# Adding the two expert rows on GpSimd, and storing the last tile in two parts

## The chip, the core and the metric

The kernel runs on one core of a Trainium2 chip. The metric is the device time of one execution, in microseconds; smaller is better. Engines go by their names in the profile: PE is TensorE (PEld its weight loads), DVE is VectorE, ACT is ScalarE, POOL is GpSimd, SP is SyncE, which here only issues DMAs.

## What is computed

One transformer block with adaptive layer norm: attention over 8 sequences of 1024 tokens with 128 features, then a mixture of 8 experts of which each token uses two, and one shared expert that every token uses. The part that matters here is the end:

```
h = relu(einsum('td,edf->tef', xf, W1) + b1)
sparse = einsum('te,tef,efd->td', combine, h, W2) + combine @ b2
shared = relu(xf @ Ws1 + bs1) @ Ws2 + bs2
x = x + gb * (sparse + shared)          # gb: one gate row for each of the 8 sequences
```

Everything is float32. `combine` has two values that are not zero in each row, so `sparse` is a sum of two expert rows per token.

## The kernel before

Tokens are laid out as 8 batches (`B`) of 1024 tokens (`S`); a batch is 8 groups (`G`) of 128 rows. In SBUF a batch of results, `res`, is 128 partitions x 1024 numbers. A tile is 512 tokens, half a batch; `K` = 4 groups.

After attention, token rows are scattered by expert to DRAM, run through the experts tile by tile, weighted, and scattered back to `rows_z` in DRAM by GpSimd's indirect DMAs (line 780, the last four on line 794). `rows_z` holds two rows for each token: the first expert's and the second's. The shared expert runs in tiles of its own, eight of them before the expert tiles and eight (batches 4 to 7, `i` = 0 to 7) after them. Those last eight tiles and the gathering of `rows_z` are the **last stage**, from about 599 us to the end.

In the last stage SP loads `rows_z` batch by batch into SBUF slots (`load_results`, line 464). A slot holds `z0`, the first experts' rows, and `z1`, the second experts' rows. The order of batches is 4, 0, 5, 1, 6, 2, 7, 3; the first half of batch 4 has a load of its own. There are six slots, and the loads of batches 7 and 3 are issued only after the third store (line 471), since they reuse the slots of batches 4 and 0.

TensorE makes a shared tile in two steps: `last_up(i)` (lines 1731 to 1733, into `score`) and `last_down(i)` (line 1940, into one of three PSUM banks `yacc`, called value or misc in the profile). ScalarE applies relu (line 967) and copies the next input (line 957, `h_hi`), VectorE makes the low part of the next input (line 1271, `last_x`), and then TensorE can start the next `last_up`.

VectorE does all the finishing, in an order written out by hand: `rows_into_result(0)`, `add_front(0)`, `last_x(5)`, `add_shared(1)`, `add_shared(2)`, `last_x(6)`, `add_front(1)`, `last_x(7)`, `add_shared(3)`, `add_shared(4)`, `add_front(2)`, `add_shared(5)`, `add_front(3)`, `add_shared(6)`, `add_last_shared(7)`. For a half batch with a shared tile (`add_shared`) these are four instructions of 128x512: PSUM + z0 (line 1640), + z1 (line 1642), times the gate `mod` (line 1643), into `res` (line 1644). For a batch without one (`add_front`, the shared part was added earlier) three of 128x1024: z0 + z1 (line 1652), gate (line 1653), into `res` (line 1654). Each waits for the one in front of it by a semaphore (`fin`). SP stores each piece when it is ready. No GpSimd instruction stands in the last stage: its last is an indirect DMA on line 794.

Of the kernel before, what the change touches and what calls it, by code (L numbers as in the profile page):

```python
# [34 lines left out]
P = 128  # L35
B, S, D = 8, 1024, 128
G = S // P
# [73 lines left out]
def adaln_moe(nc, x, c_t, wmod, w_att, b_att, wg, packs, out):  # L111
    with ExitStack() as ctx:
# [6 lines left out]
        def sem(name):  # L119
            return ctx.enter_context(nc.semaphore(name))  # L120
# [226 lines left out]
        y_sent = [sem(f"y_sent{i}") for i in range(RING)]  # L347
        z_loaded = [sem(f"z_loaded{i}") for i in range(B)]
        fin_step = sem("fin_step")
        bias_step = sem("bias_step")  # L350
# [12 lines left out]
        z_slot = {b: z_at[i % len(z_at)] for i, b in enumerate(z_order)}  # L363
        fin_parts = [p for i in range(B // 2 - 1) for p in ((B // 2 + i, 0), (i, None), (B // 2 + i, 1))]
        fin_parts += [(B // 2 - 1, None), (B - 1, 0), (B - 1, 1)]

# [24 lines left out]
        def _(sp):  # L391
# [74 lines left out]
            def store(i):  # L466

                b, half = fin_parts[i]
                sp.wait_ge(fin_ready, i + 1)
                at = slice(0, G) if half is None else slice(half * K, half * K + K)  # L470
                sp.dma_start(out_v[b, :, at.start * D:at.stop * D],
                             res[:, b * G + at.start:b * G + at.stop, :].rearrange("p g d -> p (g d)")).then_inc(stored, 16)

# [14 lines left out]
        def _(pool):  # L488
# [567 lines left out]
        def _(dve):  # L1056
# [565 lines left out]
            def rows_into_result(i):  # L1622
# [7 lines left out]
                nc.vector.tensor_tensor(r, r, z0, ALU.add).then_inc(fin_ready, 1)  # L1630

            def add_shared(i):

                b, half = divmod(FRONT + i, 2)
                dve.wait_ge(z_loaded[b], 16)
                dve.wait_ge(down_ready, FRONT + ROW_TILES + i + 1)
                z0, z1 = (z_slot[b][:, k * S + half * TILE:k * S + half * TILE + TILE].rearrange("p (g d) -> p g d", d=D) for k in range(2))
                gate = mod[:, b:b + 1, 4, :].to_broadcast([P, K, D])
                r = res[:, b * G + K * half:b * G + K * half + K, :]
                nc.vector.tensor_tensor(z0, yacc[(i + 2) % RING].rearrange("p (k d) -> p k d", k=K), z0, ALU.add).then_inc(y_evac, 1)  # L1640
                dve.wait_ge(y_evac, FRONT + ROW_TILES + i + 1)
                fin(nc.vector.tensor_tensor(z0, z0, z1, ALU.add))  # L1642
                fin(nc.vector.tensor_tensor(z0, z0, gate, ALU.mult))  # L1643
                nc.vector.tensor_tensor(r, r, z0, ALU.add).then_inc(fin_ready, 1)  # L1644

            def add_front(b):

                dve.wait_ge(z_loaded[b], 16)
                z0, z1 = (z_slot[b][:, k * S:(k + 1) * S].rearrange("p (g d) -> p g d", d=D) for k in range(2))
# [15 lines left out]

            def add_last_shared(i):

                b, half = divmod(FRONT + i, 2)
                z0, z1 = (z_slot[b][:, k * S + half * TILE:k * S + half * TILE + TILE].rearrange("p (g d) -> p g d", d=D) for k in range(2))
                gate = mod[:, b:b + 1, 4, :].to_broadcast([P, K, D])  # L1670
                r = res[:, b * G + K * half:b * G + K * half + K, :]
                fin(nc.vector.tensor_tensor(z0, z0, z1, ALU.add))
                fin(nc.vector.tensor_tensor(z0, z0, gate, ALU.mult))
                fin(nc.vector.tensor_tensor(r, r, z0, ALU.add), wait=False)
                dve.wait_ge(down_ready, FRONT + ROW_TILES + i + 1)
                nc.vector.tensor_tensor(z1, yacc[(i + 2) % RING].rearrange("p (k d) -> p k d", k=K), gate, ALU.mult).then_inc(y_evac, 1)
                dve.wait_ge(y_evac, FRONT + ROW_TILES + i + 1)
                dve.wait_ge(fin_step, fin.now())
                nc.vector.tensor_tensor(r, r, z1, ALU.add).then_inc(fin_ready, 1)
# [18 lines left out]
            add_shared(6)  # L1698
            add_last_shared(7)


        @block.tensor
        def _(pe):
# [335 lines left out]
            def last_down(i):  # L2039
                down(FRONT + ROW_TILES + i, w_shared, (i + 2) % RING, part=i % 2, banks=3)  # L2040

            pe.wait_ge(h2t_staged, 2 * B)
            last_up(0)
            last_expert_down()
            for i in range(SHARED_TILES - FRONT):
                if i + 1 < SHARED_TILES - FRONT:
                    last_up(i + 1)
                last_down(i)


# [26 lines left out]
```

## Time and profile before

| | us |
|---|---|
| median of 3 runs | 649.85 (649.65 to 651.14) |
| the profiled execution, its own time | 649.9 |
| its span (first to last instruction) | 648.2 |
| PE busy over the span | 610.2 (94%) |
| DVE busy | 460.7 (71%) |
| POOL busy | 340.9 (53%) |

The profiled execution is one run; its time outside the span is 1.7 us. Busy shares are averages over stages that have different limits, so the last stage has to be read by itself.

### The profile page before, as it was taken

How to read it: one execution, taken by the hardware profiler on the slowest of the kernel's cores; microseconds unless marked ns; L12 is line 12 of the kernel's file. 1: busy time of each engine (PE TensorE's matmuls, PEld its weight loads, DVE VectorE, ACT ScalarE, POOL GpSimd, SP SyncE). 2: the span in 40 equal slices, each digit the busy share in tenths (PEclk: the TensorE clock that was granted, in tenths of full speed). 3: DMA queues.
4: the chain of work that ended last, by engine and by line, in shares of the span. 5: the costliest groups of instructions: out<-in, count | busy, mean ns of one | idle time of the engine just before them, and what ended most of it. 6: DMA issues, size and time to landing. Idle time of an engine off the chain costs nothing.

```text
span 648.2 us, 12495 instructions
## 1 busy us (share of the span) xinstructions
PE 610.2 (94%) x4311; PEld 557.4 (86%) x4311; DVE 460.7 (71%) x1415; ACT 397.6 (61%) x635; POOL 340.9 (53%) x341
## 2 busy tenths in 40 slices
PE   3898999999999998986999999999999999999995
PEld 2587988898889897875998999999999999999995
DVE  7889878798989898996775564544545445453788
ACT  3588787878787876554345555565655656555441
POOL 4531614766666666777560575555655556656000
PEclk9899999999999999997999999999999999999998
DMA  7140000111111111111166456656666566601972
GB/s 296 38 163 2 1 1 10 38 33 34 35 34 34 34 39 35 40 47 45 64 197 201 149 175 207 187 178 199 196 204 198 180 196 194 204 31 34 360 305 113
DMA packets 29902, 76.67 MB, mean 118 GB/s; under 512 B 7126, under 2 KB 11374, under 8 KB 29712
## 3 DMA queue, kind: packets, MB, share of 16 engines
q1 hardware_dynamic: 20480, 58.49, 27.2%
q0 software_dynamic: 8640, 16.93, 7.7%
q8 instruction: 34, 0.56, 0.4%
q10 hardware_dynamic: 720, 0.47, 0.2%
q14 instruction: 28, 0.23, 0.1%
HBM read 53.53 MB, written 23.24 MB: 118 GB/s over the span
## 4 chain that ended last, share of the span: by engine, by line
PE 49%; DVE 3%; issue 1%; ACT 1%; ACTq 0%
PE value L1940 18%; PE misc L1940 7%; PE score L1731 7%; PE score L1733 7%; PE score L1732 7%; PE value L1991 2%; PE misc L1772 1%; PE value L2030 1%; DVE res L1644 0%; DVE rows_all L1155 0%; ACT work L967 0%; DVE rows_all L1642 0%; DVE rows_all L1643 0%; DVE rows_all L1640 0%; DVE w_ring L1653 0%
## 5 line engine op out<-in xcount | busy, mean ns | idle before, releaser
L780 POOL DMA_INDIRECT rows_z<-tile_y,tags x138 | 139.2, 1009 | 115.1 <-DVE tile_y L1560 49.5
L1731 PE MATMUL score<-h_hi,h_lo 128*128 128x512 f32 (+1 forms) x252 | 93.8, 372 | 2.2 <-DVE h_hi L1271 1.9
L1759 PE MATMUL value<-w_ring,work 128*128 128x129 f32 x768 | 92.1, 276 | 1.1 <-ACT work L840 1.0
L1759 PEld LDWEIGHTS value<-w_ring,work 128*128 128x128 f32 x768 | 89.6, 192 | 3.2 <-ACT work L840 1.4
L967 ACT ACTIVATE work<-score,w_ring 128x512 f32<-128x512 f32 (+1 forms) x96 | 53.0, 614 | 60.8 <-PE score L1733 59.2
L1733 PE MATMUL score<-h_hi,h_lo 128*128 128x512 f32 (+1 forms) x252 | 88.7, 352 | 0.0
L1732 PE MATMUL score<-h_hi,h_lo 128*128 128x512 f32 (+1 forms) x252 | 88.4, 351 | 0.0
L576 POOL DMA_INDIRECT rows_x<-work,slot x64 | 65.1, 1017 | 39.7 <-issue 15.5
L838 ACT ACTIVATE work<-work 128x1024 f32<-128x1024 f32 x64 | 67.2, 1050 | 26.4 <-DVE work L1168 26.2
L1168 DVE TENSOR_TENSOR work<-score,lw 128x1024 f32<-128x1024 f32 x64 | 76.6, 1214 | 1.9 <-PE score L1733 1.2
L967 ACT ACTIVATE work<-score,w_shared 128x512 f32<-128x512 f32 x64 | 40.3, 684 | 49.9 <-PE score L1733 48.5
L840 ACT ACTIVATE work<-work 128x1024 f32<-128x1024 f32 x64 | 67.8, 1060 | 2.0
L967 ACT ACTIVATE work<-score,rows_all 128x256 f32<-128x256 f32 (+1 forms) x92 | 43.8, 547 | 38.6 <-PE score L1733 37.8
L1731 PE MATMUL score<-q_hi,h_lo 128*128 128x512 f32 x128 | 54.6, 426 | 5.5 <-DVE work L1168 4.9
L1731 PEld LDWEIGHTS score<-h_hi,h_lo 128*128 128x128 f32 x252 | 47.7, 189 | 7.8 <-DVE rows_all L1177 2.0
L1733 PEld LDWEIGHTS score<-h_hi,h_lo 128*128 128x128 f32 x252 | 47.4, 188 | 6.6
L1732 PEld LDWEIGHTS score<-h_hi,h_lo 128*128 128x128 f32 x252 | 47.7, 189 | 4.9
L1733 PE MATMUL score<-q_hi,h_hi 128*128 128x512 f32 x128 | 50.8, 397 | 0.0
L1732 PE MATMUL score<-q_lo,h_hi 128*128 128x512 f32 x128 | 50.6, 396 | 0.0
L1940 PEld LDWEIGHTS value<-w_shared,work 128*128 128x128 f32 x416 | 49.5, 197 | 1.1 <-ACT work L967 0.5
L1940 PE MATMUL value<-w_shared,work 128*128 128x128 f32 x416 | 50.2, 281 | 0.0
L1275 DVE TENSOR_TENSOR h_lo<-w_ring,h_lo 128x512 fp32r<-128x512 f32 x24 | 16.6, 692 | 43.5 <-ACT h_lo L960 43.5
(254 smaller groups left out, 1270.7 us busy)
## 6 DMA issues: line engine op xcount, KB each, us to landing
w_ring<-packs SPq DMA_DIRECT2D x24, 578.0 KB, 3.9
rows_all<-packs SPq DMA_DIRECT2D x23, 578.0 KB, 3.9
lw<-rows_x SPq DMA_DIRECT2D x24, 260.0 KB, 3.8
res<-x SPq DMA_DIRECT2D x8, 512.0 KB, 6.2
h_t<-rows_z SPq DMA_DIRECT2D x3, 1024.0 KB, 10.4
mod<-mod_rows SPq DMA_DIRECT2D x1, 2560.0 KB, 10.0
rows_z<-tile_y,tags POOLq DMA_INDIRECT x142
rows_all<-rows_z SPq DMA_DIRECT2D x2, 1024.0 KB, 12.9
```

The lines of the kernel that those rows point to most:

```text
L576: nc.gpsimd.indirect_dma_start(rows_x[:, :], bass.IndirectOffsetOnAxis(ap=slot[b % 2][:, k, g:g + 1], axis=0), (rows_1, rows_2)[k][b % 2][ ...
L780: nc.gpsimd.indirect_dma_start(rows_z[:, :], bass.IndirectOffsetOnAxis(ap=tags[pos][:, k, 0:1].bitcast(I32), axis=0), tile_y[par][:, k, :] ...
L838: nc.scalar.activation(prob[:, t % 4, :], prob[:, t % 4, :], ACT.Tanh).then_inc(tanh_done, 1)
L840: nc.scalar.activation(prob[:, t % 4, :], prob[:, t % 4, :], ACT.Exp).then_inc(exp_done, 1)
L967: ins = nc.scalar.activation(hidden[par][:, c, 0:rows], score[:, c, 0:rows], ACT.Relu, bias=w[:, B1_AT + c:B1_AT + c + 1])
L1168: nc.vector.tensor_tensor(prob[:, t % 4, :].rearrange("p (h n) -> p h n", h=2), score[:, 2 * (t % 2):2 * (t % 2) + 2, :], lw[:, at:at + S] ...
L1275: nc.vector.tensor_tensor(w1_lo[par], w[:, 0:F], w1_hi[par].bitcast(F32), ALU.subtract).then_inc(w_split, 1)
L1731: nc.tensor.matmul(out, a_lo, b_hi, start=True, stop=False)
L1732: nc.tensor.matmul(out, a_hi, b_lo, start=False, stop=False)
L1733: return nc.tensor.matmul(out, a_hi, b_hi, start=False, stop=True)
L1759: ins = nc.tensor.matmul(value[:, s // 3, c0:c0 + D + 1], prob[:, t % 4, s * P:(s + 1) * P], normal[b % 3][:, t, :], start=(t == 0 and s % ...
L1940: ins = nc.tensor.matmul(yacc[par][:, k * D:(k + 1) * D], hidden[part][:, c, k * P:(k + 1) * P], w[:, W2_AT + c * D:W2_AT + (c + 1) * D], ...
```

## The change

GpSimd gets eight instructions at the end of its program, `sum_rows`: z0 = z0 + z1 for batch 0, the second half of batch 4, and batches 5, 1, 6, 2, 7, 3, each as soon as its load has landed. VectorE no longer adds z1; it waits for the sum (`z_summed`) instead. (The first half of batch 4, `rows_into_result`, keeps its addition on VectorE.) The last shared tile is made by TensorE in two parts of two groups each, the second into the bank `xt_ps`, which is free by then; VectorE gates, adds and SP stores each part by itself.

```diff
-        fin_parts += [(B // 2 - 1, None), (B - 1, 0), (B - 1, 1)]
+        fin_parts += [(B // 2 - 1, 0, G), (B - 1, 0, K), (B - 1, K, K + 2), (B - 1, K + 2, G)]
...
+            def sum_rows(b, n0=0):
+                pool.wait_ge(z_loaded[b], 16)
+                z0, z1 = (z_slot[b][:, k * S + n0:(k + 1) * S] for k in range(2))
+                nc.gpsimd.tensor_tensor(z0, z0, z1, ALU.add).then_inc(z_summed, 1)
+            sum_rows(z_order[1])
+            sum_rows(z_order[0], TILE)
+            for b in z_order[2:]:
+                sum_rows(b)
...
+            def summed(b):
+                dve.wait_ge(z_summed, 1 + (z_order[1:2] + z_order[0:1] + z_order[2:]).index(b))
...
             def add_shared(i):
-                dve.wait_ge(z_loaded[b], 16)
+                summed(b)
...
                 nc.vector.tensor_tensor(z0, yacc[(i + 2) % RING].rearrange("p (k d) -> p k d", k=K), z0, ALU.add).then_inc(y_evac, 1)
                 dve.wait_ge(y_evac, FRONT + ROW_TILES + i + 1)
-                fin(nc.vector.tensor_tensor(z0, z0, z1, ALU.add))
                 fin(nc.vector.tensor_tensor(z0, z0, gate, ALU.mult))
                 nc.vector.tensor_tensor(r, r, z0, ALU.add).then_inc(fin_ready, 1)
...
             def add_front(b):
-                dve.wait_ge(z_loaded[b], 16)
+                summed(b)
...
-                fin(nc.vector.tensor_tensor(z0, z0, z1, ALU.add))
                 fin(nc.vector.tensor_tensor(z0, z0, gate, ALU.mult))
                 nc.vector.tensor_tensor(r, r, z0, ALU.add).then_inc(fin_ready, 1)
...
+            def last_shared_part(i, part, bank):
+                dve.wait_ge(*((down_ready, FRONT + ROW_TILES + i + 1) if part else (part_ready, 1)))
+                n = K // 2
+                gated = nc.vector.tensor_tensor(z1, bank[:, 0:n * D].rearrange("p (k d) -> p k d", k=n), mod[:, b:b + 1, 4, :].to_broadcast([P, n, D]), ALU.mult)
+                gated.then_inc(part_evac, 1)
+                dve.wait_ge(part_evac, part + 1)
+                nc.vector.tensor_tensor(r, r, z1, ALU.add).then_inc(fin_ready, 1)
...
-            add_last_shared(7)
+            last_rows_into_result(7)
+            last_shared_part(7, 0, yacc[(7 + 2) % RING])
+            last_shared_part(7, 1, xt_ps)
```

On VectorE, from the finishing of batch 0 (`add_front(0)`) to that of the second half of batch 4 (`add_shared(1)`), before (h2_t, which the profile calls h_t, is where the slots of batches 4 and 0 lie):

```order
L1652 TENSOR_TENSOR h2_t<-h2_t 128x1024 [waits z_loaded0]
L1653 TENSOR_TENSOR h2_t<-h2_t,mod 128x1024 [waits fin_step]
L1654 TENSOR_TENSOR res<-res,h2_t 128x1024 [waits fin_step]
L1271 TENSOR_TENSOR h_hi0<-h2_t,h_hi0 128x512 [waits x_hi_ready]
L1640 TENSOR_TENSOR h2_t<-value,h2_t 128x512 [waits down_ready,z_loaded4]
L1642 TENSOR_TENSOR h2_t<-h2_t 128x512 [waits y_evac]
L1643 TENSOR_TENSOR h2_t<-h2_t,mod 128x512 [waits fin_step]
L1644 TENSOR_TENSOR res<-res,h2_t 128x512 [waits fin_step]
```

The same place after the change:

```order
L1669 TENSOR_TENSOR h2_t<-h2_t,mod 128x1024 [waits z_summed]
L1670 TENSOR_TENSOR res<-res,h2_t 128x1024 [waits fin_step]
L1285 TENSOR_TENSOR h_hi0<-h2_t,h_hi0 128x512 [waits x_hi_ready]
L1658 TENSOR_TENSOR h2_t<-value,h2_t 128x512 [waits down_ready,z_summed]
L1660 TENSOR_TENSOR h2_t<-h2_t,mod 128x512 [waits y_evac]
L1661 TENSOR_TENSOR res<-res,h2_t 128x512 [waits fin_step]
```

One instruction of each group is gone, and the first of each group waits for GpSimd's sum and no longer for the load. On GpSimd, what stands at the end of the program after the change, behind the last indirect DMAs:

```order
L796 DMA rows_z<-tile_y1,tags4 16384x128 [waits y_ready]
L804 TENSOR_TENSOR h2_t<-h2_t 128x1024 [waits z_loaded0]
L804 TENSOR_TENSOR h2_t<-h2_t 128x512 [waits z_loaded4]
L804 TENSOR_TENSOR work<-work 128x1024 [waits z_loaded5]
L804 TENSOR_TENSOR rows_all<-rows_all 128x1024 [waits z_loaded1]
L804 TENSOR_TENSOR rows_all<-rows_all 128x1024 [waits z_loaded6]
L804 TENSOR_TENSOR w_ring<-w_ring 128x1024 [waits z_loaded2]
L804 TENSOR_TENSOR h2_t<-h2_t 128x1024 [waits z_loaded7]
L804 TENSOR_TENSOR h2_t<-h2_t 128x1024 [waits z_loaded3]
```

Before, the program ended with the DMA. On VectorE, the end of the program, before:

```order
L1672 TENSOR_TENSOR h2_t<-h2_t 128x512
L1673 TENSOR_TENSOR h2_t<-h2_t,mod 128x512 [waits fin_step]
L1674 TENSOR_TENSOR res<-res,h2_t 128x512 [waits fin_step]
L1676 TENSOR_TENSOR h2_t<-value,mod 128x512 [waits down_ready]
L1679 TENSOR_TENSOR res<-res,h2_t 128x512 [waits fin_step,y_evac]
```

and after:

```order
L1688 TENSOR_TENSOR h2_t<-h2_t,mod 128x512 [waits z_summed]
L1689 TENSOR_TENSOR res<-res,h2_t 128x512 [waits fin_step]
L1699 TENSOR_TENSOR h2_t<-value,mod 128x256 [waits part_ready,fin_step]
L1702 TENSOR_TENSOR res<-res,h2_t 128x256 [waits part_evac]
L1699 TENSOR_TENSOR h2_t<-value,mod 128x256 [waits down_ready]
L1702 TENSOR_TENSOR res<-res,h2_t 128x256 [waits part_evac]
```

The addition is gone, and the two last instructions of 128x512 are four of 128x256.

## Rows read from the trace of the kernel before

**Rows 1.** Stretches: length, busy of PE, PEld, DVE, ACT, POOL; clock, DMA, GB/s
```profile
606.20:621.20 15.00, 15.00 (x100) 13.60 (x100) 14.56 (x18) 7.30 (x12) 0.00 (x0) 1.00 1.02 406
621.20:623.20 2.00, 2.00 (x20) 2.00 (x19) 0.04 (x2) 1.85 (x4) 0.00 (x0) 1.00 1.02 416
623.20:645.70 22.50, 17.90 (x136) 16.75 (x134) 21.83 (x28) 5.07 (x8) 0.00 (x0) 0.96 0.39 156
```

**Rows 2.** Timeline of DVE in the last stage: start, length, engine, line
```profile
617.48 1.22 DVE L1652 TENSOR_TENSOR rows_all<-rows_all 128x1024 f32<-128x1024 f32 x1
618.73 1.23 DVE L1653 TENSOR_TENSOR rows_all<-rows_all,mod 128x1024 f32<-128x1024 f32 x1
...
623.18 0.69 DVE L1271 TENSOR_TENSOR h_hi<-h_t,h_hi 128x512 fp32r<-128x512 f32 x1 [1.96 <-ACT h_hi L957]
623.79 0.68 DVE L1640 TENSOR_TENSOR work<-misc,work 128x512 f32<-128x512 f32 x1
624.51 0.69 DVE L1642 TENSOR_TENSOR work<-work 128x512 f32<-128x512 f32 x1
625.23 0.69 DVE L1643 TENSOR_TENSOR work<-work,mod 128x512 f32<-128x512 f32 x1
...
644.27 0.68 DVE L1676 TENSOR_TENSOR h_t<-value,mod 128x512 f32<-128x512 f32 x1
644.99 0.69 DVE L1679 TENSOR_TENSOR res<-res,h_t 128x512 f32<-128x512 f32 x1
```

**Rows 3.** Timeline of PE: the last shared tile's down projection
```profile
637.37 3.74 PE L1940 MATMUL value<-w_shared,work 128*128 128x128 f32 x32
```

**Rows 4.** Timelines of POOL and DVE, 46 to 52 us
```profile
46.99 4.70 POOL L550 TENSOR_TENSOR res<-res,mod 128x1024 f32<-128x1024 f32 x2
...
48.15 1.24 DVE L1075 SCALAR_TENSOR_TENSOR shift<-moments,rstd 128x8 f32<-128x8 f32 x1
49.32 1.21 DVE L1168 TENSOR_TENSOR work<-score,lw 128x1024 f32<-128x1024 f32 x1
50.45 1.28 DVE L1075 SCALAR_TENSOR_TENSOR shift<-moments,rstd 128x24 f32<-128x24 f32 x1
```

**Rows 5.** Lengths of single lines over the whole span, min/median/max ns
```profile
L1075 DVE SCALAR_TENSOR_TENSOR shift<-moments,rstd x5: 167/383/1281, 10.1 to 85.3; 128x8 f32<-128x8 f32 x3, 128x24 f32<-128x24 f32 x1, 128x16 f32<-128x16 f32 x1
...
L554 POOL TENSOR_SCALAR rstd<-moments x8: 238/534/583, 67.8 to 295.9; 128x8 f32<-128x8 f32 x8
```

**Rows 6.** Timeline of DVE and POOL around 99 us
```profile
99.34 0.66 DVE L1116 TENSOR_TENSOR h_lo<-tile_y,h_hi 128x512 fp32r<-128x512 f32 x1
...
99.61 0.49 POOL L554 TENSOR_SCALAR rstd<-moments 128x8 f32<-128x8 f32 x1 [16.55 <-DVE moments L1065]
```

**Rows 7.** Lengths of POOL's 128x1024 additions, min/median/max ns
```profile
L550 POOL TENSOR_TENSOR res<-res,mod x8: 2367/2381/2399, 47.0 to 247.3; 128x1024 f32<-128x1024 f32 x8
...
L571 POOL TENSOR_TENSOR row<-row,mod x1: 2192/2192/2192, 75.2 to 75.2; 128x1024 f32<-128x1024 f32 x1
```

**Rows 8.** Timeline of DVE: a 128x256 read of PSUM in the expert stage
```profile
591.65 0.42 DVE L1603 TENSOR_TENSOR tile_y<-value,rows_all 128x256 f32<-128x256 f32 x1 [2.92 <-PE value L2030]
592.11 0.48 DVE L1608 TENSOR_SCALAR tile_y<-tile_y,tags 128x128 f32<-128x128 f32 x2
```

**Rows 9.** DMA issues in the last stage: count, KB, us to landing
```profile
h_t<-rows_z SPq DMA_DIRECT2D x1, 1024.0 KB, 6.0
...
w_ring<-rows_z SPq DMA_DIRECT2D x1, 1024.0 KB, 17.1
...
h_t<-rows_z SPq DMA_DIRECT2D x1, 1024.0 KB, 10.4
...
out<-res SPq DMA_DIRECT2D x1, 256.0 KB, 2.0
```

**Rows 10.** Timeline of SP: issues of the loads in the last stage
```profile
599.75 1.43 SPq L464 DMA_DIRECT2D h_t<-rows_z  x3
...
602.82 0.52 SPq L464 DMA_DIRECT2D w_ring<-rows_z  x1
```

More of the change, by code:

```diff
@@ L466, in store @@
             def store(i):
-                b, half = fin_parts[i]
+                b, g0, g1 = fin_parts[i]
                 sp.wait_ge(fin_ready, i + 1)
-                at = slice(0, G) if half is None else slice(half * K, half * K + K)
-                sp.dma_start(out_v[b, :, at.start * D:at.stop * D],
-                             res[:, b * G + at.start:b * G + at.stop, :].rearrange("p g d -> p (g d)")).then_inc(stored, 16)
+                sp.dma_start(out_v[b, :, g0 * D:g1 * D],
+                             res[:, b * G + g0:b * G + g1, :].rearrange("p g d -> p (g d)")).then_inc(stored, 16)
             load_results(z_order[0], z_half_loaded, 0, TILE)
@@ L1664, in _, with last_rows_into_result @@
             last_expert()
-            def add_last_shared(i):
+            def last_rows_into_result(i):
                 b, half = divmod(FRONT + i, 2)
-                z0, z1 = (z_slot[b][:, k * S + half * TILE:k * S + half * TILE + TILE].rearrange("p (g d) -> p g d", d=D) for k in range(2))
-                gate = mod[:, b:b + 1, 4, :].to_broadcast([P, K, D])
+                summed(b)
+                z0 = z_slot[b][:, half * TILE:half * TILE + TILE].rearrange("p (g d) -> p g d", d=D)
                 r = res[:, b * G + K * half:b * G + K * half + K, :]
[L1672 to L1678, printed above, removed]
+                fin(nc.vector.tensor_tensor(z0, z0, mod[:, b:b + 1, 4, :].to_broadcast([P, K, D]), ALU.mult))
+                fin(nc.vector.tensor_tensor(r, r, z0, ALU.add))
+            def last_shared_part(i, part, bank):
+                b, half = divmod(FRONT + i, 2)
+                dve.wait_ge(*((down_ready, FRONT + ROW_TILES + i + 1) if part else (part_ready, 1)))
+                n = K // 2
+                z1 = z_slot[b][:, S + part * n * D:S + (part + 1) * n * D].rearrange("p (g d) -> p g d", d=D)
+                g0 = b * G + K * half + n * part
+                r = res[:, g0:g0 + n, :]
+                gated = nc.vector.tensor_tensor(z1, bank[:, 0:n * D].rearrange("p (k d) -> p k d", k=n), mod[:, b:b + 1, 4, :].to_broadcast([P, n, D]), ALU.mult)
+                gated.then_inc(part_evac, 1)
+                dve.wait_ge(part_evac, part + 1)
                 nc.vector.tensor_tensor(r, r, z1, ALU.add).then_inc(fin_ready, 1)
@@ L2040, in last_down, with last_down_in_parts @@
                 down(FRONT + ROW_TILES + i, w_shared, (i + 2) % RING, part=i % 2, banks=3)
+            def last_down_in_parts(i):
+                n = FRONT + ROW_TILES + i
+                pe.wait_ge(y_evac, n - 2)
+                pe.wait_ge(hidden_ready, HALVES * (n + 1))
+                for part, bank in enumerate((yacc[(i + 2) % RING], xt_ps)):
+                    for c in range(C):
+                        for k in range(K // 2):
+                            at = (K // 2 * part + k) * P
+                            ins = nc.tensor.matmul(bank[:, k * D:(k + 1) * D], hidden[i % 2][:, c, at:at + P],
+                                                   w_shared[:, W2_AT + c * D:W2_AT + (c + 1) * D],
+                                                   start=(c == 0 and k == 0), stop=(c == C - 1), skip_group_check=True)
+                    ins.then_inc(down_ready if part else part_ready, 1)
             pe.wait_ge(h2t_staged, 2 * B)
@@ L2044, in _ @@
             last_expert_down()
-            for i in range(SHARED_TILES - FRONT):
-                if i + 1 < SHARED_TILES - FRONT:
-                    last_up(i + 1)
+            for i in range(SHARED_TILES - FRONT - 1):
+                last_up(i + 1)
                 last_down(i)
+            last_down_in_parts(SHARED_TILES - FRONT - 1)
 def kernel(**inputs):
```

9 lines of the change are left out of this document (6 added, 3 removed).

## The prediction

> **What bounds the kernel now.** I first cut the last stage into stretches [rows 1]. TensorE is busy throughout until about 641 us; VectorE is busy for 14.56 of 15 us, then idle for 2 us (it waits for ScalarE, which follows TensorE's pace), then busy for 21.83 of the last 22.5 us. GpSimd does nothing. So from 623.2 us on VectorE sets the end, and before that it is just in time. Its timeline says the same [rows 2]: the 1.96 us wait in front of line 1271 is the last idle time, and from there to 645.68 (644.99 + 0.69) each instruction starts as soon as the one before it lets it. The last matmul group ends at 637.37 + 3.74 = 641.1 us [rows 3], 4.6 us before VectorE is done. After VectorE comes only the last store, 2.0 us [rows 9], and 0.5 us to the end of the span at 648.2.
>
> VectorE work removed after 623.2 us is therefore worth its full time until TensorE's end is reached; work removed before it only widens the idle time, unless something has filled that up.
>
> **What the change removes.** Steps are counted from start to start [rows 2]. A 128x512 addition on line 1642 takes 625.23 - 624.51 = 0.72 us; there are six of them and one like them on line 1672. A 128x1024 addition on line 1652 takes 618.73 - 617.48 = 1.25 us; there are four. Together 7 x 0.72 + 4 x 1.25 = 10.0 us. Of this 4 x 0.72 + 2 x 1.25 + 0.72 = 6.1 us stand behind 623.2.
>
> **What it adds on VectorE.** Now two last instructions take 0.72 + 0.69 = 1.41 us. Two parts take, with 0.42 us for a 128x256 instruction and 0.46 from its start to a next one that waits for it [rows 8], and 0.08 us less than its length where the next one does not wait (623.18 to 623.79 is 0.61 against 0.69 [rows 2]): 0.46 + 0.34 + 0.46 + 0.42 = 1.68, so +0.27. In front of them one `res` addition is now waited for, 0.72 in place of 0.61: +0.11. Sum +0.4 us. It buys something only if VectorE reaches the last tile before TensorE does.
>
> **What it adds on GpSimd, and the main term.** Seven sums of 128x1024 and one of 128x512. The nearest rows are GpSimd's own 128x1024 float32 additions: 2.38 us in one form, 2.19 in another [rows 7]. Neither has two plain operands; I take 2.3 and keep both ends. The half sum is not in the trace; it lies between half of 2.3 and all of it, and I take 1.25, near the half, since most of such a length should go with the elements.
>
> On the face of it these 17.4 us run beside VectorE. The trace says they do not. At 48.15 us VectorE starts a tiny instruction, 128x8 from two SBUF tensors, while GpSimd's addition runs. It takes 1.24 us [rows 4]; the shortest on that line takes 0.167 [rows 5]. It ends at 49.39, and GpSimd's first addition ends at 46.99 + 2.35 = 49.34. The next one at 50.45 takes 1.28 us and ends at 51.73; GpSimd's second addition ends at 51.69. Between them, under the second of these GpSimd additions, VectorE multiplies 128x1024 numbers from PSUM with others from SBUF in 1.21 us (line 1168) and is not held up [rows 4]. So an instruction of VectorE with two SBUF inputs waits until GpSimd's is over, and one with an input in PSUM does not. The reverse is there as well: GpSimd's line 554 takes 0.49 us when it starts under a 128x512 VectorE subtraction from SBUF that ends at 100.00 [rows 6], and 0.238 alone [rows 5]; it ends 0.10 us after VectorE's.
>
> The Trainium skill has this as a rule ("SBUF — State Buffer", section "SBUF: two separate sides"): VectorE and GpSimd share a pair of SBUF ports that is locked for a whole instruction, against VectorE instructions with two SBUF inputs too. By that rule the trace agrees, in both directions. Its "GPSIMD Engine Reference", section 3.1, gives 4497 ns for an addition of 2048 float32; half of that, an estimate of 2.25 us, would make the sum 0.35 us smaller.
>
> In the last stage only lines 1640 and 1676 read PSUM. Everything else on VectorE (lines 1271, 1643, 1644, 1653, 1654, and what is left of the rest) has two SBUF inputs.
>
> Price of one sum in a dense stretch: it gets in at the gap between two VectorE instructions. GpSimd's record then ends 0.10 + 2.3 - 0.24 = 2.16 us after the VectorE record in front of it; the next VectorE instruction begins its work 0.13 us before that (51.69 against 51.73 - 0.167 = 51.56 [rows 4, 5]), in place of 0.03 us after its predecessor. Loss 2.16 - 0.13 - 0.03 = 2.0 us. Half sum 0.95. Three of the eight meet a VectorE instruction that would have overlapped its predecessor by 0.08, +0.3 in all. Eight sums: 7 x 2.0 + 0.95 + 0.3 = 15.25 us.
>
> What covers them: each time a line-1640 instruction (0.72 us a step) falls under a sum, that much is not lost. I laid the two programs side by side, each taking turns, with the loads landing as now: batch 0 is there at 606.2 (the second of three issues from 599.75 on, at about 600.2, and 6.0 us), batch 2 at 602.8 + 17.1 = 619.9 [rows 9, 10], the other three between. Two of the sums, those of batches 6 and 7, fall on a line-1640 instruction: -1.4 us. The idle 1.96 us at 621.2 is eaten: -1.96.
>
> **Sum.** -10.0 + 0.4 + 15.25 - 1.4 - 1.96 = +2.3 us. VectorE ends at 648.0, TensorE well before it, and the time is 649.9 + 2.3 = **652.2 us**; the profiled execution's 649.9 is also the median of the runs (649.85).
>
> **What is late next.** By 621 us six sums have been run, 12.9 us of them against about 4 us removed, so VectorE is some 7 to 9 us late there. The third store comes at about 623, not 614, and behind it in SP's queue are the loads of batches 7 and 3. They landed 10.4 us after issue beside other traffic [rows 9]; on an idle DMA I expect about 5 and 8 us, so they are there near 628 and 631, and VectorE needs them at 640 or later: no cost. Line 1271 for tile 6 comes near 625.4, and TensorE would have started that tile at 624.7: TensorE waits for about 0.8 us and ends near 642, still under VectorE. Stores run behind VectorE as before, and two small ones replace the last: the last one 128 KB in place of 256 KB, taken as no gain.
>
> **Rivals.**
>
> 1. *The additions run free* (the engines do not stand in each other's way for these shapes). Then VectorE loses 10.0 us of work and TensorE bounds the end: the last group at 641.1, VectorE's last pieces by 642.1 to 642.7, so -3.0 us, **646.9**. For it: removed work stands where VectorE is the bound. Against it: rows 4 to 6. The sign turns where the sums cost VectorE, after cover, what it saves: 10.0 - 0.4 + 1.96 = 11.6 us in place of my 13.85, or 1.5 us a full sum in place of 1.8. Chance 0.10.
>
> 2. *VectorE keeps its turn in a dense stretch*, and GpSimd gets in only under a PSUM instruction or when VectorE waits for a sum. Then more of the sums are covered (five or six, not two) but VectorE waits for some: by the same side-by-side layout +1.2 us, **651.1**. The trace has no GpSimd addition that arrives in such a chain of long instructions, so it is open. Chance 0.10.
>
> 3. *The turns as forecast*: 0.80, its own range 650.4 to 654.4. Its bounds: 2.19 or 2.40 us a sum move the result by -0.8 or +0.7; no cover at all by line 1640 is +1.4, and two more covered sums -1.4; a longer tie-up at the start of each sum (up to 0.14 us, the part that I take to run before it needs the ports) +1.1.
>
> 4. *The two-part store does nothing*: part of case 3, not another one; it costs 0.4 us there and would save up to 1 us in case 1.
>
> **How the numbers follow.** About 0.3% (2 us) is what a measurement of this kernel can tell from no change: faster is under 647.9, slower over 651.8. Case 3 lies around 652.2 with a spread of about 1.2 us: 0.62 of it is slower, 0.36 within, 0.02 faster. Case 2: 0.3 slower, 0.65 within. Case 1: nearly all faster. Sums: slower 0.53, within 0.36, faster 0.11. The range is 649.8 to 654.6: it leaves out case 1 (0.10), and about 0.1 at the ends.
>
> **What would show it.** In the profile of the changed kernel: (a) GpSimd has eight records on line 804; those that start under a VectorE instruction are longer than 2.3 us. (b) Eight VectorE records with two SBUF inputs are stretched, by up to 2.1 us, each ending its own usual length, less 0.13 us, after a GpSimd record's end; the records that read PSUM stay at 0.68. (c) The idle 1.96 us is gone. (d) The third store is issued near 623 us. (e) VectorE ends about 6 us behind TensorE. I am wrong if VectorE's 128x512 records keep 0.69 us under a sum (case 1), or if GpSimd's records are stretched and VectorE's are not (case 2), or if a sum takes 4 us.

## The result, and the profile after

The changed kernel takes **653.55 us** (653.32 to 654.79) against 649.84 (649.65 to 651.45) for the one before: ratio 1.0039, 95% interval 1.0026 to 1.0053, 3.7 us slower. The profiled execution's own time is 653.32 us, its span 651.6.

The stretches of the last stage, the first two with the bounds of [rows 1], the third from 623.2 up to 649.0, 0.4 us before VectorE's end. Columns: length, busy time of PE, PEld, DVE, ACT, POOL (with instructions), granted clock, DMA share, GB/s.

```profile
606.20:621.20 15.00, 15.00 (x105) 13.75 (x104) 14.83 (x9) 6.17 (x11) 12.73 (x5) 1.00 0.95 374
621.20:623.20 2.00, 2.00 (x15) 1.80 (x14) 1.97 (x3) 1.90 (x4) 2.00 (x2) 1.00 0.14 56
...
623.20:649.00 25.80, 19.28 (x146) 17.96 (x144) 25.25 (x28) 6.15 (x10) 6.36 (x3) 0.93 0.55 201
```

VectorE is now "busy" for the whole of the two microseconds in which it used to be idle, but in the first 15 us it gets through 9 instructions in place of 18. A good part of its busy time here is time in which an instruction is held up. GpSimd's timeline shows its sums (start, length, engine, line, tensors, how many; in brackets the idle time in front and what ended it).

```profile
607.34 4.08 POOL L804 TENSOR_TENSOR h_t<-h_t 128x1024 f32<-128x1024 f32 x2 [7.78 <-DMA h_t<-rows_z]
612.55 3.45 POOL L804 TENSOR_TENSOR work<-work 128x1024 f32<-128x1024 f32 x1 [1.14 <-DMA work<-rows_z]
615.97 5.61 POOL L804 TENSOR_TENSOR rows_all<-rows_all 128x1024 f32<-128x1024 f32 x2
621.55 2.81 POOL L804 TENSOR_TENSOR w_ring<-w_ring 128x1024 f32<-128x1024 f32 x1
628.04 2.82 POOL L804 TENSOR_TENSOR h_t<-h_t 128x1024 f32<-128x1024 f32 x1 [3.69 <-DMA h_t<-rows_z]
631.76 2.38 POOL L804 TENSOR_TENSOR h_t<-h_t 128x1024 f32<-128x1024 f32 x1 [0.90 <-DMA h_t<-rows_z]
```

VectorE's timeline in the same stage, with the columns of [rows 2], of which six of the eight long records and the end are shown:

```profile
607.43 2.85 DVE L1644 TENSOR_TENSOR res<-res,h_t 128x512 f32<-128x512 f32 x1
610.20 2.29 DVE L1669 TENSOR_TENSOR h_t<-h_t,mod 128x1024 f32<-128x1024 f32 x1
612.53 1.23 DVE L1670 TENSOR_TENSOR res<-res,h_t 128x1024 f32<-128x1024 f32 x1
613.67 2.89 DVE L1285 TENSOR_TENSOR h_hi<-h_t,h_hi 128x512 fp32r<-128x512 f32 x1
...
619.37 2.76 DVE L1661 TENSOR_TENSOR res<-res,h_t 128x512 f32<-128x512 f32 x1
622.06 0.68 DVE L1658 TENSOR_TENSOR work<-value,work 128x512 f32<-128x512 f32 x1
622.77 2.14 DVE L1660 TENSOR_TENSOR work<-work,mod 128x512 f32<-128x512 f32 x1
...
632.05 2.64 DVE L1660 TENSOR_TENSOR work<-work,mod 128x512 f32<-128x512 f32 x1
...
648.97 0.42 DVE L1702 TENSOR_TENSOR res<-res,h_t 128x256 f32<-128x256 f32 x1
```

Read the two together. GpSimd's sum of batch 2 runs from 621.55 to 624.36. VectorE's line 1658, which reads PSUM, runs under it in its usual 0.68 us; the next, line 1660 with two SBUF inputs, takes 2.14 us in place of 0.69 and ends at 624.91, 0.55 us after the sum. The sum that starts at 612.55 takes 3.45 us in place of 2.38 (the last one, at 631.76, finds the way free): it started under a VectorE instruction that ran until 613.76, and got going after it. There are eight long VectorE records; they lose 2.16, 1.06, 2.20, 1.45, 2.07, 1.45, 2.18 and 1.95 us against their usual lengths, 14.5 us together. VectorE never waits for a sum here (the waits of this stage have none for GpSimd), so all that the sums cost it lies inside these records.

**Where 3.4 us of the profile went.** I measure the stage from the start of the first instruction that drains a shared tile (`w_ring<-misc,mod`) to the end of VectorE's last. Before, that is 599.69 to 645.68 us, 46.0; after, 600.82 to 649.39, 48.6. So 2.6 us are lost in the stage. The time from VectorE's end to the end of the span is 0.3 us shorter (the last store is 128 KB, not 256). The remaining 1.1 us are lost before the stage begins, and they appear at one place: up to 280 us the changed kernel is 0.2 us ahead of the other, from VectorE's next instruction on (280.83 us before, 281.82 now, where it waits 1.11 us for TensorE) 1.0 us behind, and 1.1 when the stage begins. It is the end of this stretch, first in the changed kernel:

```profile
275.00:280.00 5.00, 4.83 (x29) 4.77 (x29) 3.69 (x34) 4.94 (x7) 3.10 (x4) 0.67 0.14 44
```

and the same stretch in the kernel before:

```profile
275.00:280.00 5.00, 4.83 (x42) 4.66 (x42) 3.72 (x33) 4.94 (x7) 3.15 (x4) 1.00 0.13 42
```

TensorE was granted 0.67 of its speed there against 1.00, and did 29 matmuls in place of 42 in the same busy time. A mean of 0.67 over 5 us is part of the stretch at 2.4 GHz and part at 1.2. The changed instructions all stand some 320 us later. The unchanged kernel, profiled again below, was granted 0.90 in this stretch and 0.76 in the next; `combined` below, which has no sums, was granted 0.66 in it; `after_again`, the changed kernel once more, 1.00 in it and 0.66 from 285 to 290 us. So such a dip needs no sum, and the unchanged kernel has them too. Still, all six runs of the changed kernel are slower than the 2.3 us of the stage and its end explain, by some 1.4 us at the medians. Whether that part comes with the new program or with this set of runs stays open.

### The profile page after: what moved, and what is told of

Its sections match the earlier page's. It is cut to its first block, busy times and chain, and to the rows that moved or that the text cites. A ratio compares the mean times of both kernels' runs of the same rounds, so it can differ in the third digit from the quotient of the medians.

```text
span 651.6 us, 12495 instructions
## 1 busy us (share of the span) xinstructions
PE 611.8 (94%) x4311; PEld 557.8 (86%) x4311; DVE 466.4 (72%) x1406; ACT 397.8 (61%) x635; POOL 362.5 (56%) x349
## 4 chain that ended last, share of the span: by engine, by line
PE 46%; DVE 6%; issue 1%; ACT 0%; ACTq 0%
PE value L1965 17%; PE misc L1965 7%; PE score L1756 6%; PE score L1758 6%; PE score L1757 6%; PE value L2016 2%; DVE h_hi L1285 1%; DVE work L1660 1%; PE misc L1797 1%; PE value L2055 1%; DVE h_t L1669 1%; DVE h_t L1660 0%; DVE res L1644 0%; DVE res L1661 0%; DVE rows_all L1169 0%
## 5 line engine op out<-in xcount | busy, mean ns | idle before, releaser
L1784 PE MATMUL value<-w_ring,work 128*128 128x129 f32 x768 | 93.6, 279 | 2.0 <-ACT work L854 1.9
L1784 PEld LDWEIGHTS value<-w_ring,work 128*128 128x128 f32 x768 | 91.2, 195 | 4.3 <-ACT work L854 2.6
L1965 PEld LDWEIGHTS value<-w_shared,work 128*128 128x128 f32 x384 | 46.1, 198 | 1.1 <-ACT work L981 0.5
L1965 PE MATMUL value<-w_shared,work 128*128 128x128 f32 x384 | 46.7, 281 | 0.1
```

The lines of the kernel that those rows point to most:

```text
L1784: ins = nc.tensor.matmul(value[:, s // 3, c0:c0 + D + 1], prob[:, t % 4, s * P:(s + 1) * P], normal[b % 3][:, t, :], start=(t == 0 and s % ...
L1965: ins = nc.tensor.matmul(yacc[par][:, k * D:(k + 1) * D], hidden[part][:, c, k * P:(k + 1) * P], w[:, W2_AT + c * D:W2_AT + (c + 1) * D], ...
```

## The experiments

The unchanged kernel's own time differs between the sets of runs (649.8, 657.5, 658.3, 657.7, 651.7 us); each kernel is compared with the unchanged one inside its own set. "Stage" is the length just defined.

### The changed kernel again, and its two halves (second set, before: 657.46 us)

`after_again` is the changed kernel as it is.

> The changed kernel once more. Theory A (shared port): the last stage costs 2.3 us more than before, whatever happens ahead of it. Besides, the first profile showed TensorE's clock granted at 0.67 between 275 and 280 us, where the profile of before had 1.00, and everything behind it 1.1 us later. If that belongs to the change, this run has it again and comes out at 653.4; if it comes and goes, some runs are near 652.2 and the profile may be without it.

It took 661.88 us: ratio 1.0085 (1.0051 to 1.0119), 4.4 us more, where 2.3 was expected for the last stage. The stage is 49.0 us, against 44.6 for the unchanged kernel in the third set (it wasn't profiled in the second) and 44.9 for `parts_only` in the same set. Nearly all of the 4.4 us lies in the stage, so the 1.1 us ahead of it are not there again. The loss is larger than the 2.6 of the first set, and VectorE's timeline says where. The unchanged kernel (`before_again`, third set) waits for loads early in the stage, and not for ScalarE later:

```profile
615.62 0.69 DVE L1628 TENSOR_TENSOR h_t<-h_t 128x512 f32<-128x512 f32 x1 [1.43 <-DMA h_t<-rows_z]
...
618.20 1.23 DVE L1652 TENSOR_TENSOR h_t<-h_t 128x1024 f32<-128x1024 f32 x1 [0.44 <-DMA h_t<-rows_z]
```

The changed kernel waits for the sum at that second place:

```profile
618.28 1.22 DVE L1669 TENSOR_TENSOR h_t<-h_t,mod 128x1024 f32<-128x1024 f32 x1 [2.95 <-POOL h_t L804]
```

Here the idle 1.96 us of [rows 2] isn't there to be eaten, and the first sum stands fully in VectorE's way: VectorE waits 2.95 us for it, where it waited 0.44 for the load. The other seven sums stretch VectorE's records by 11.8 us together. With the 10.0 us removed and the 0.4 added that is +4.7, against 4.4 measured. The mechanism is the same, the cover is gone.

`sums_only` keeps the sums and stores the last tile whole:

```diff
-        fin_parts += [(B // 2 - 1, 0, G), (B - 1, 0, K), (B - 1, K, K + 2), (B - 1, K + 2, G)]
+        fin_parts += [(B // 2 - 1, 0, G), (B - 1, 0, K), (B - 1, K, G)]
...
-            last_shared_part(7, 0, yacc[(7 + 2) % RING])
-            last_shared_part(7, 1, xt_ps)
+            last_shared_whole(7)
```

> Only the eight sums on GpSimd, last tile whole. Theory A: all of the loss is here: the changed kernel less 0.3 us, 653.2 (or 652.0 where the 1.1 us are missing). Rival (the parts carry the loss): 650 or less.

662.49 us, ratio 1.0073 (1.0044 to 1.0102), stage 48.9: the loss of the changed kernel, and the 0.3 us by which it was to be less can't be told in these runs. `parts_only` is the reverse, the kernel before with the last tile in two parts:

> Only the two-part last tile, all sums on VectorE. Theory A: VectorE is still 4.6 us behind TensorE, so the parts only add 0.3 to 0.4 us: 650.2. Rival (smaller last pieces shorten the end): 649.4 or less. Rival on the 1.1 us ahead of the last stage (it comes with any change of this program): 651.3.

657.34 us, ratio 1.0006 (0.9984 to 1.0028); stage 44.9, then 2.2 us to the end in place of 2.5. Its 0.3 us more on VectorE and 0.3 us less behind it cancel. The whole loss belongs to the sums.

`no_sums` takes the eight GpSimd instructions out of the changed kernel and lets VectorE wait for the loads; VectorE's instructions are those of the changed kernel. It leaves out the second experts' rows (but for the first half of batch 4).

```diff
-            sum_rows(z_order[1])
-            sum_rows(z_order[0], TILE)
-            for b in z_order[2:]:
-                sum_rows(b)
...
-                dve.wait_ge(z_summed, 1 + (z_order[1:2] + z_order[0:1] + z_order[2:]).index(b))
+                dve.wait_ge(z_loaded[b], 16)
```

> Leaves the second experts' rows out of the result (except in the first half of batch 4): neither engine adds them; everything else as in the changed kernel. VectorE's instruction stream is that of the changed kernel, with no GpSimd instruction beside it. Theory A: no VectorE record is stretched and TensorE bounds the end: 646.9. Rival (VectorE's 10 us less are lost to waits for loads or TensorE in any case): 649 or more.

654.27 us, ratio 0.9948 (0.9922 to 0.9974), 3.2 us less than before. No VectorE record is long, and VectorE waits for the others now:

```profile
629.75 0.69 DVE L1281 TENSOR_TENSOR h_hi<-h_t,h_hi 128x512 fp32r<-128x512 f32 x1 [3.23 <-ACT h_hi L967]
...
644.21 0.69 DVE L1654 TENSOR_TENSOR h_t<-misc,h_t 128x512 f32<-128x512 f32 x1 [1.77 <-PE misc L1961]
```

The stage is 41.6 us, 3.0 less than before and 7.4 less than with the sums. This is the end that rival 1 priced at -3.0 us: 10 us of VectorE work are worth 3, since TensorE comes next. It doesn't yet say whether the 7.4 us come from GpSimd's reading and adding, or from VectorE's waiting for it.

### Which part of a GpSimd instruction holds VectorE (third and fourth set)

`before_again` is the unchanged kernel, for a profile in this set.

> The kernel before once more, for a profile beside the others of this set. Theory A: no VectorE record of 128x512 with two SBUF inputs is longer than 0.75 us in the last stage, and from the first shared tile's evacuation to VectorE's end there are about 46 us. Nothing is changed, so the time is that of before.

658.41 us beside 658.3, ratio 0.9982 (0.9956 to 1.0008); stage 44.6, where I had expected the 46 of the first set. No record is long.

`write_only` is the changed kernel, but puts two instructions (IOTA, which writes a row of counting numbers) in the place of each sum, the second waiting for the first, that only write to z1 and read nothing. The waits between the engines stay. It leaves out the second experts' rows.

```diff
-                nc.gpsimd.tensor_tensor(z0, z0, z1, ALU.add).then_inc(z_summed, 1)
+                z1 = z_slot[b][:, S + n0:2 * S]
+                nc.gpsimd.iota(z1, pattern=[[1, S - n0]], base=0, channel_multiplier=0, allow_small_or_imprecise_dtypes=True).then_inc(z_first, 1)
+                first[0] += 1
+                pool.wait_ge(z_first, first[0])
+                nc.gpsimd.iota(z1, pattern=[[1, S - n0]], base=0, channel_multiplier=0, allow_small_or_imprecise_dtypes=True).then_inc(z_summed, 1)
```

> Leaves the second experts' rows out (except in the first half of batch 4). In place of each sum GpSimd runs two iotas over the same 1024 (or 512) numbers, which write SBUF and read nothing, about 2.1 us together; VectorE waits for them as it did for the sums. Theory A in the form that reads are what is locked: VectorE is not stretched, TensorE bounds the end, about 3 us less than before. Rival A2 (any access of GpSimd blocks VectorE for its length): eight times about 1.6 us, so about the time of before, and VectorE records of 1.4 us or more. Rival B (VectorE is only slow because it waits for GpSimd's result): also about 3 us less, since GpSimd is as long busy here as with the sums.

653.71 us, ratio 0.9944 (0.9919 to 0.997); stage 41.8, as without any sums. GpSimd works from 630.15 to 632.20:

```profile
630.15 0.98 POOL L807 IOTA w_ring<- 128x1024 f32 x1 [1.66 <-DMA w_ring<-rows_z]
631.21 0.99 POOL L810 IOTA w_ring<- 128x1024 f32 x1
```

and VectorE, in the same time, is not touched:

```profile
630.28 0.69 DVE L1291 TENSOR_TENSOR h_hi<-h_t,h_hi 128x512 fp32r<-128x512 f32 x1 [1.74 <-ACT h_hi L977]
630.88 0.68 DVE L1664 TENSOR_TENSOR work<-misc,work 128x512 f32<-128x512 f32 x1
631.60 0.69 DVE L1666 TENSOR_TENSOR work<-work,mod 128x512 f32<-128x512 f32 x1
```

So GpSimd's presence and its writes stretch no VectorE record. The waits are there (VectorE waits 2.9 us for the first pair), but VectorE, with 10 us less to do, has that time to spare before TensorE. What stretches VectorE's records comes with GpSimd's reading. Rival B forecast the same time, so the time doesn't refute it; the records of the changed kernel do, since they are long with no wait for GpSimd between them. By the Trainium skill ("SBUF — State Buffer", "SBUF: two separate sides"), a VectorE instruction with two SBUF inputs contends with a GpSimd instruction that reads SBUF and not with one that only writes; by that rule, this trace agrees.

`one_input` (fourth set, before: 657.73 us) is the changed kernel, but multiplies z1 by one in place of the sum: one input, one output. It leaves out the second experts' rows too.

```diff
-                nc.gpsimd.tensor_tensor(z0, z0, z1, ALU.add).then_inc(z_summed, 1)
+                nc.gpsimd.tensor_scalar(z1, z1, 1.0, None, ALU.mult).then_inc(z_summed, 1)
```

> Leaves the second experts' rows out (except in the first half of batch 4). In place of each sum GpSimd multiplies z1 by 1.0, one SBUF input, one output. Theory A: GpSimd's read is what shuts VectorE out, so VectorE records with two SBUF inputs are stretched again, each to the end of a GpSimd record, though GpSimd needs only one input; how much the time changes depends on the length of that record, which no profile so far shows. Rival A3 (only GpSimd's second read port collides, so one input is free): no VectorE record over 1.3 us, and the time that the kernel with no sums had.

654.57 us, ratio 0.9959 (0.9937 to 0.9981), stage 41.9. One of GpSimd's instructions,

```profile
633.93 3.15 POOL L804 TENSOR_SCALAR w_ring<-w_ring 128x1024 f32<-128x1024 f32 x1
```

and VectorE around it:

```profile
633.23 1.21 DVE L1669 TENSOR_TENSOR rows_all<-rows_all,mod 128x1024 f32<-128x1024 f32 x1
634.48 1.94 DVE L1670 TENSOR_TENSOR res<-res,rows_all 128x1024 f32<-128x1024 f32 x1
636.34 0.68 DVE L1285 TENSOR_TENSOR h_hi<-h_t,h_hi 128x512 fp32r<-128x512 f32 x1
```

GpSimd's record goes on until 637.08, with about 2.8 us of its own (5.57 us for two in a row), but VectorE loses only 1.94 - 1.22 = 0.72 us to it, and runs free under the rest. Other 128x512 records under such an instruction take 1.41 us, again 0.72 more; seven records are longer than usual, by 0.12 to 0.83 us, 4.2 us together. With two inputs VectorE lost 2.1 us to a sum of 2.38. So the price isn't set by how long GpSimd's record is. Theory A and its rival both missed: the records are stretched (against A3), but not to the end of GpSimd's (against theory A). The time doesn't show these 4.2 us, since here too TensorE comes next. The Trainium skill's rule (same section) is that the shared pair goes to whoever starts first for the whole instruction; by that rule, as far as the lengths of GpSimd's records can be trusted, the trace agrees for two inputs and disagrees for one.

### Fewer sums, or sums made elsewhere

`one_sum` (third set) is the kernel before with a single sum on GpSimd, that of batch 2, which was to fall where VectorE had idle time:

```diff
+            on_pool = (2,)
+            for b in on_pool:
+                sum_rows(b)
```

> Only batch 2's sum on GpSimd, last tile whole, all else as before. Its load lands at about 19 us into the last stage, just ahead of VectorE's idle 1.96 us. Theory A: VectorE is held up once, for 2.1 us, which that idle time covers, and add_front(2) behind it is 1.25 us shorter: 1.1 us less than before. Rival (a sum costs more than it saves wherever it stands): 0.8 us more than before.

658.49 us, ratio 1.001 (0.9986 to 1.0033); stage 44.8. GpSimd:

```profile
628.64 2.91 POOL L806 TENSOR_TENSOR w_ring<-w_ring 128x1024 f32<-128x1024 f32 x1 [21.90 <-DMA w_ring<-rows_z]
```

and VectorE:

```profile
629.94 2.16 DVE L1668 TENSOR_TENSOR work<-work 128x512 f32<-128x512 f32 x1
```

The sum takes 1.25 us from VectorE and puts 1.47 on it; the rest of its 2.1 or so is covered by the PSUM-reading instruction in front of this record. Neither expectation came true, the time is that of before: I had taken the cover (the 1.96 us idle) from the profile of the first set, and in this set it isn't there.

`dma_add` (third set) has no sum on GpSimd. For batches 6, 2, 7 and 3, a second DMA adds z1 onto z0 as it arrives, issued by GpSimd; `dma_add_two` (fourth set) does so for 7 and 3 alone. Both have the last tile in two parts.

```diff
+                pool.wait_ge(z_loaded[b], 16)
+                nc.gpsimd.dma_start(z_slot[b][:, 0:S], z_v[b][:, 1, :], accum_op=ALU.add).then_inc(z_added[on_pool.index(b)], 16)
```

> Batches 6, 2, 7 and 3: SP loads only the first experts' rows, and GpSimd issues a DMA for each that adds the second experts' rows to them in SBUF on the way; no engine computes those sums. The others are added on VectorE as before; last tile in two parts. Theory A: VectorE loses 6.1 us of work behind its idle time, no port is taken by a computing GpSimd, TensorE bounds the end: about 3 us less than before. Rival (an adding DMA is slow, or GpSimd's building of its descriptors holds VectorE up): the rows come late or VectorE records are stretched, and the time is that of before or more.

657.14 us, ratio 0.9998 (0.9971 to 1.0025); stage 44.9. No VectorE record is long. The waits view of VectorE for the stage has (us in total, times, longest):

```profile
DVE h_t L1682 <- DMA h_t<-rows_z: 2.5, 1, 2.5
DVE rows_all L1665 <- DMA rows_all<-rows_z: 1.6, 1, 1.6
...
DVE w_ring L1682 <- DMA w_ring<-rows_z: 1.0, 1, 1.0
```

and the DMA issues say why (count, KB, us from issue to landing):

```profile
h_t<-rows_z POOLq DMA_DIRECT2D x2, 512.0 KB, 10.4
...
w_ring<-rows_z POOLq DMA_DIRECT2D x1, 512.0 KB, 10.5
```

Each half-size transfer takes 8.8 to 10.5 us, and is issued only when the plain one in front of it has landed. While they run, the DMA engines are as busy and move less; two stretches of this kernel, ahead of the adding and during it (last two columns DMA share and GB/s):

```profile
625.00:630.00 5.00, 5.00 (x35) 4.52 (x34) 4.92 (x6) 3.05 (x5) 1.87 (x2) 1.00 1.02 408
...
635.00:640.00 5.00, 5.00 (x37) 4.64 (x36) 3.85 (x5) 1.32 (x4) 0.86 (x1) 1.00 1.06 263
```

VectorE's 5.4 us of additions (two of 1.25 and four of 0.72, by the steps of [rows 2]) turned into 5.1 us of waiting: the rival came true, in that the rows come late. (The 6.1 us of the expectation counted the second half of batch 5, which VectorE still adds here.)

> Adding DMAs for batches 7 and 3 only, VectorE adds the rest, last tile in two parts. With four such DMAs VectorE waited 5.2 us for rows that landed 8 to 10 us after issue. Theory A: with two, issued when the other loads are done, they land in 6 us or less and VectorE waits little: 2.7 us of additions gone, 0.4 added by the parts, about 2 us less than before. Rival (an adding DMA lands late in any case): within 1 us of before.

656.14 us, ratio 0.9979 (0.996 to 0.9999); stage 42.7, 1.9 less than `before_again`. The forecast of about 2 us holds; the interval of the time by itself ends just short of 1. Of those three waits only a small one is left:

```profile
643.80 1.23 DVE L1682 TENSOR_TENSOR h_t<-h_t,mod 128x1024 f32<-128x1024 f32 x1 [0.37 <-DMA h_t<-rows_z]
```

`pe_adds` (fourth set) is the kernel before; for tiles 4, 5 and 6 TensorE adds z1 onto the tile in PSUM by a matmul with the identity, and VectorE's line 1642 is left out there.

```diff
+                    ins = nc.tensor.matmul(yacc[par][:, :], ident[:, :], z_slot[b][:, S + half * TILE:S + half * TILE + TILE],
+                                           start=False, stop=True, skip_group_check=True)
```

> The kernel before, but for tiles 4, 5 and 6 TensorE adds z1 into the tile's PSUM bank with one more matmul against the identity (128x512), and VectorE leaves its addition out. Theory A: VectorE is the bound at the end by 4.6 us; it loses 3 x 0.72 = 2.2 us, TensorE gets 3 x 0.45 = 1.35 us: 1.5 to 2.2 us less than before. Rival (TensorE's longer work becomes the bound or the identity matmul costs more, 1 us or more each): no gain.

658.09 us, ratio 0.9998 (0.9982 to 1.0014); stage 44.7. TensorE's timeline:

```profile
634.13 1.02 PE L1948 MATMUL value<-rows_all,ident 128*128 128x512 f32 x2
634.59 0.80 PE L1733 MATMUL score<-h_hi,h_lo 128*128 128x512 f32 x1
635.23 0.40 PE L1734 MATMUL score<-h_hi,h_lo 128*128 128x512 f32 x1
```

The float32 matmul of 512 columns stands as two records (x2), and TensorE ends 42.6 us after the stage's start in place of 40.0: 2.6 / 3 = 0.86 us a tile, where I had expected 0.45, and more than the 0.72 that VectorE saves. VectorE then waits for TensorE, 0.6 and 1.4 us. The work went to the engine that was next in line, and made it the bound.

### The smaller moves, together (fifth set, before: 651.67 us)

`combined`: `dma_add_two`, with batches 3 and 7 swapped in the order of loading and adding, and the identity matmul for tile 4 alone. VectorE's own order is unchanged: it takes batch 3 (`add_front(3)`) before batch 7 (`add_shared(6)`), so the swap brings first the rows that are needed first. The expectation below has this the wrong way round ("7 is drained before 3").

```diff
+            PE_ADDS = (4,)
+            z_order[-2:] = z_order[:-3:-1]
...
+            on_pool = (3, 7)
```

> Before, with no sum on GpSimd: two DMAs that add (batches 3 and 7, the one for batch 3 issued first and batches 7 and 3 swapped in the order so that 7 is drained before 3), tile 4 (first half of batch 6) taking its first expert's rows by an identity matmul on TensorE, and the last tile in two parts. Theory: with the two adding DMAs alone VectorE ended 42.7 us after the first shared tile's evacuation began, TensorE being done at 40.0; the swap takes away the 0.37 us that VectorE waited for a late row block, the identity matmul takes one 0.72 us pass from VectorE and puts 0.86 us on TensorE, so VectorE ends 41.7 to 41.9 us after that mark in place of the 44.6 of the kernel before, and the time falls by 2.7 to 2.8 us (0.4%). Rival: the rows of the second adding DMA land late again (VectorE waits for DMA by 0.5 us or more), and the end stays at 42.7: 0.2% less time than before. Second rival: TensorE becomes the bound in the last tiles (VectorE waits for PE by over 0.5 us), with the same 0.2%.

**648.80 us** (647.61 to 649.17), ratio 0.995 (0.9936 to 0.9964), 2.9 us less than before. The adding DMAs are issued early enough:

```profile
624.68 0.99 POOL L809 DMA_DIRECT2D h_t<-rows_z  x1 [25.41 <-DMA h_t<-rows_z]
625.95 0.86 POOL L809 DMA_DIRECT2D h_t<-rows_z  x1 [0.28 <-DMA h_t<-rows_z]
```

and the waits view of VectorE for the stage (us in total, times, longest) has no wait for a DMA any more:

```profile
DVE h_hi L1289 <- ACT h_hi L975: 5.1, 2, 3.1
DVE h_t L1667 <- PE misc L1983: 1.0, 1, 1.0
```

The gain is that of the theory, but its lengths were not: the stage is 44.0 us, where I had expected 41.7 to 41.9 from the sets two to four. So the agreement of the time is in part luck. This set looks like the first one (the stage starts at 600.52 us, TensorE ends 42.3 us into it, 0.9 after the 41.4 of the kernel before, as the matmul's price says), so the 46.0 of the first set is the better thing to hold it against: -2.0 us in the stage, -0.3 behind it. The -2.0 adds up: -2.7 us of additions made by DMA, -0.7 by the matmul, +0.4 for the parts, +1.0 of waiting for TensorE. The unchanged kernel wasn't profiled in this set, so the split of the 2.9 us isn't shown.

Nor is it shown that each move helped. The adding DMA of batch 3 is issued at 624.68 and lands 5.4 us later, that of batch 7 at 625.95 and lands 7.7 later, by 633.7; VectorE takes batch 3 at 635.89, so here either order would have been in time. The second rival is half true: VectorE waits 1.0 us for TensorE in front of tile 6:

```profile
637.14 1.23 DVE L1685 TENSOR_TENSOR res<-res,h_t 128x1024 f32<-128x1024 f32 x1
639.34 0.69 DVE L1667 TENSOR_TENSOR h_t<-misc,h_t 128x512 f32<-128x512 f32 x1 [0.97 <-PE misc L1983]
```

An estimate from these rows: without the matmul VectorE would have come to tile 6 at about 638.3 + 0.72 = 639.0, and TensorE would have had it ready at 639.34 - 0.86 = 638.5. So the matmul rather cost 0.3 us than brought anything; no run has the DMAs and the swap without it. More taken from VectorE ahead of tile 6 would no longer help. Behind it some 0.8 us are left: VectorE starts on the last part at 643.64 us, and TensorE is done at 642.80.

## Why the prediction was right

Forecast 652.2 us (649.8 to 654.6), measured 653.55; "slower" had 0.53. The step that decided it holds: a VectorE instruction with two SBUF inputs stands still while GpSimd adds, so that what looks like free time on GpSimd is VectorE's time. Point by point:

- **The price of a sum.** The undisturbed sum takes 2.38 us, where I took 2.3. Four full sums that nothing covered cost 2.16, 2.20, 2.07 and 2.18 us, against 2.0 and the 0.1 or so for an overlap lost; the half sum 1.06, against 0.95.
- **The cover by line 1640 (now 1658).** I counted two sums, those of batches 6 and 7, 1.4 us. These two have none (2.07 and 2.18); three others have some, those of batches 1, 2 and 3, which cost 1.45, 1.45 and 1.95, about 1.6 us less than without. The side-by-side layout had the wrong sums, and that its total is near is luck. All long records together 14.5 us, where the forecast's 15.25 - 1.4 gives 13.85.
- **What is removed and what the parts add.** Both held: `parts_only` shows the +0.3 us of the parts by themselves, and that they bring 0.3 back behind VectorE, which I had taken as nothing.
- **The idle time was eaten**, as (c) said: VectorE is busy for 1.97 us of the 2. The sum of the terms as measured, -10.0 + 0.4 + 14.5 - 2.0, gives +2.9; the stage grew by 2.6. Of the 0.3 between them, 0.15 is a gap in front of an earlier line 1271 that I hadn't counted.
- **What is late.** SP's timeline:

```profile
610.31 12.19 SPq L473 DMA_DIRECT2D out<-res  x3
622.54 0.99 SPq L467 DMA_DIRECT2D h_t<-rows_z  x2
```

  The third store is out by 622.5, forecast 623, and the loads of batches 7 and 3 right behind it. Their sums start when they land, at 628.04 and 631.76; forecast 628 and 631. These clock times hold the 1.1 us that were lost ahead of the stage; counted from its start, the store is 1.6 us earlier than forecast and the two sums 1.1 and 0.4. VectorE needs them later, so that the loads are late costs nothing. TensorE did wait before tile 6, by 0.3 us where the forecast has 0.8:

```profile
626.34 0.47 PE L1756 MATMUL score<-h_hi,h_lo 128*128 128x512 f32 x1 [0.30 <-issue]
...
639.04 3.74 PE L2076 MATMUL value<-w_shared,work 128*128 128x128 f32 x32
```

  It ended at 642.78, forecast 642 (42.0 us into the stage, 0.5 later than before), and VectorE 6.6 us behind it, forecast about 6.
- **(b)** held for all eight records, up to 2.20 us where I said 2.1.
- **Small slips** in the working: six sums by 621 us are 5 x 2.3 + 1.25 = 12.75 us, not 12.9; and in the last stage line 1617 reads PSUM too, ahead of all sums. Neither changes the forecast.
- **Rival 1** (the additions run free) is refuted by the long records, and its size confirmed by `no_sums`: -3.2 us. **Rival 2** (VectorE keeps its turn) wasn't seen: GpSimd's sum got in at the first gap after the VectorE instruction under which it started.
- **What I had not forecast** are the 1.1 us lost before the last stage, in a stretch (275 to 280 us) with a lower granted clock. Without them the forecast of this profile would have been less than 0.1 us off; part of that agreement is luck, since the sums after cover were 0.65 us too cheap, the store 0.3 us too dear, and the stage grew by 0.3 us less than its terms add up to.
- **What the forecast depended on without saying so**: the idle 1.96 us. In the second set it wasn't there, and the same change cost 4.4 us.

## What to carry to other kernels

Before work goes to an idle GpSimd, look at what VectorE runs at that time: if its instructions have two SBUF inputs, price a two-input GpSimd instruction at nearly its whole length on VectorE, less what VectorE does from PSUM in the meantime. Here a 1.25 us addition became a 2.1 us one. Look next at the engine that is second: of 10 us taken off VectorE about 3 came back in the stage (`no_sums`), since TensorE was that close behind; the 2.9 us that `combined` gains came with 3.4 us of additions moved, most of them to DMAs that had time to land, and the part that went to TensorE probably brought nothing, since TensorE was the next bound. And an idle time that is to cover a cost belongs to one execution: check in a second set of runs that it is there.

## What the runs showed of the hardware that I had not expected

- A one-input GpSimd instruction (128x1024 float32) takes 2.8 us, longer than the two-input sum at 2.38, and holds a VectorE instruction with two SBUF inputs for 0.72 us; the two-input sum holds it for 2.1. I have no run that tells why.
- A DMA that adds into SBUF takes 6.5 to 10.5 us for 512 KB (medians of the issues), and 263 GB/s were moved in such a stretch, 408 in one without, with the DMA engines equally busy (share 1.06 and 1.02). GpSimd's own part in issuing it (0.86 to 0.99 us) didn't hold VectorE up.
- An identity matmul of 128x512 in float32 stands as two records and costs TensorE 0.86 us.
